# Gated attention stage: where the output projection is accumulated, and its place among the products

## The reference, cut to what matters

```python
def _L1_attn_ref(query, Wq, bq, Wk, bk, Wv, bv, Wu, bu, Wo, bo, ln_w, ln_b):
    q = jax.nn.relu(_heads(query @ Wq + bq))
    k = jax.nn.relu(_heads(query @ Wk + bk))
    v = _heads(query @ Wv + bv)
    u = query @ Wu + bu
    kv = jnp.einsum('bhnd,bhne->bhde', k, v)
    kv = _abs_clamp(kv)
    out = jnp.einsum('bhnd,bhde->bhne', q, kv)
    out = out.transpose(0, 2, 1, 3).reshape(query.shape)
    mu = jnp.mean(out, axis=-1, keepdims=True)
    var = jnp.var(out, axis=-1, keepdims=True)
    out = (out - mu) * jax.lax.rsqrt(var + EPS) * ln_w + ln_b
    out = u * out
    return out @ Wo + bo
...
x = x + _L1_attn_ref(_layernorm(x, axis=-1), ...)
```

## Time and profile before

| | us |
| --- | --- |
| median of 3 runs | 2989.97 (2986.45 to 2991.01) |
| the profiled execution | 2985.77 |
| its span in the trace | 2984.0 |
| PE busy in the span | 2905.4 (97%) |
| VectorE, ScalarE, GpSimd busy | 2340.0, 1729.2, 1743.0 |
| gated stage | about 2667 to 2867 in the trace |

### The profile page before, as it was taken

The page is one execution under the profiler, slowest core; times in us unless marked ns, Lnnn a source line. Parts: engine busy times, 40 slices in busy tenths (PEclk is TensorE's granted clock), DMA queues, the critical chain, the costliest instruction groups (busy, mean ns, idle before and its releaser), DMA issues.

```text
span 2984.0 us, 95481 instructions
## 1 busy us (share of the span) xinstructions
PE 2905.4 (97%) x34222; PEld 2534.5 (85%) x34222; DVE 2340.0 (78%) x6541; ACT 1729.2 (58%) x4568; POOL 1743.0 (58%) x1948
## 2 busy tenths in 40 slices
PE   6999999999999999999999999999999999999999
PEld 5888888878888888887888888878888888888888
DVE  6888887677778887888777787777777877887977
ACT  4777752267778324776777772247777622554355
POOL 7878740078888234334888861048888455627632
PEclk9999999999999999999999999999999999999999
DMA  4121121011211101000121112111211200000001
GB/s 143 45 75 42 47 82 37 27 33 41 71 40 43 49 21 44 11 12 23 36 71 40 41 47 72 35 29 40 69 42 43 65 22 14 29 0 1 1 15 43
DMA packets 178763, 122.65 MB, mean 41 GB/s; under 512 B 27532, under 2 KB 175336, under 8 KB 178024
## 3 DMA queue, kind: packets, MB, share of 16 engines
q1 hardware_dynamic: 177432, 117.77, 14.7%
q10 hardware_dynamic: 1104, 1.90, 0.2%
HBM read 48.29 MB, written 20.98 MB: 23 GB/s over the span
## 4 chain that ended last, share of the span: by engine, by line
PE 82%; DVE 6%; POOL 5%; issue 3%; SPq 1%; DMA 1%; ACT 1%; DVEq 0%; POOLq 0%; ACTq 0%
PE bank L406 7%; PE bank L408 7%; PE bank L407 7%; PE pair_bank L616 6%; PE scores L568 5%; PE scores L406 5%; PE scores L407 5%; PE scores L408 5%; PE bank L534 3%; PE pair_bank L406 2%; PE pair_bank L887 2%; PE pair_bank L886 2%; PE pair_bank L885 2%; PE scores L834 2%; PE scores L833 2%
## 5 line engine op out<-in xcount | busy, mean ns | idle before, releaser
L2956 POOL TENSOR_TENSOR prob<-prob,rsum 128x384 f32<-128x384 f32 x504 | 447.1, 914 | 226.6 <-DVE rsum L2114 226.6
L1395 ACT ACTIVATE prob<-prob,nmax 128x192 f32<-128x192 f32 x1024 | 451.9, 443 | 152.1 <-DVE nmax L2108 152.1
L1636 ACT ACTIVATE gate<-scores,bias 128x512 f32<-128x512 f32 x192 | 132.1, 688 | 499.3 <-PE scores L408 499.2
L2943 POOL TENSOR_TENSOR rn<-ss,mhalf 128x16 f32<-128x16 f32 x120 | 351.9, 2932 | 10.0
L406 PE MATMUL bank<-wqkv_hi,hT_hi 128*128 128x512 f32 x768 | 332.9, 434 | 7.3 <-DVE rot_t L2063 4.5
L2950 POOL TENSOR_TENSOR qk<-rot_t 128x512 f32<-128x512 f32 x256 | 322.5, 1280 | 12.2 <-DVE ss L2075 7.7
L2108 DVE CUSTOM_DVE_ANT_0 prob<-scores,masks,rn 128x192 f32<-128x192 f32 x768 | 267.4, 413 | 66.8 <-PE scores L568 65.3
L408 PE MATMUL bank<-wqkv_hi,hT_lo 128*128 128x512 f32 x768 | 304.2, 396 | 0.0
L407 PE MATMUL bank<-wqkv_lo,hT_hi 128*128 128x512 f32 x768 | 302.1, 393 | 0.0
L2924 POOL TENSOR_TENSOR rstd<-meanvar,eps 128x4 f32<-128x4 f32 x48 | 11.0, 229 | 486.3 <-DVE meanvar L2013 486.3
L406 PE MATMUL scores<-gT_hi,w_hi 128*128 128x512 f32 x576 | 227.6, 395 | 1.7 <-DVE gT_lo L2358 1.3
(11 more groups left out here) (415 smaller groups left out, 9562.9 us busy)
## 6 DMA issues: line engine op xcount, KB each, us to landing
Vlo<-V SPq DMA_DIRECT2D x256, 64.0 KB, 2.0
Vhi<-V SPq DMA_DIRECT2D x256, 64.0 KB, 2.0
H<-Y SPq DMA_DIRECT2D x128, 64.0 KB, 1.8
H<-ya SPq DMA_DIRECT2D x128, 64.0 KB, 1.9
yb<-Y SPq DMA_DIRECT2D x128, 64.0 KB, 1.6
HB<-Y SPq DMA_DIRECT2D x32, 256.0 KB, 2.8
HB<-yb SPq DMA_DIRECT2D x32, 256.0 KB, 3.0
raw<-in_L_ffn_wqkv SPq DMA_DIRECT2D x4, 1536.0 KB
```

The lines of the kernel that those rows point to most:

```text
L1395: e.activation(pb, pb, ACT.Exp, bias=nm[r][:, x:x + 1], scale=-1.0, accum_out=sums[r][:, x:x + 1]).then_inc(s_acEX[gi], 1)
L2943: e.tensor_tensor(rn[u][:, :], ss[u % 2][:, :], mhalf[:, :], ALU.pow).then_inc(s_plRN, 1)
L2956: e.tensor_tensor(pair, pair, rs[:, 2 * gi:2 * gi + 2].unsqueeze(2).to_broadcast([P, 2, KW]), ALU.mult).then_inc(s_plPN[gi], 1)
```

## The change

The projection of tiles 0 to 20 now goes into the right half (columns 256 to 511) of bank 6 or 7, the one that does not hold the product of its own parity, instead of bank 5. PE therefore waits ahead of it for `o_` of that bank's product instead of for `u_` and `X`; `u_` no longer waits for `X`; and `out_` of tiles 3 to 23 waits until VectorE has added the projection that lies in its bank. PE takes `kv` ahead of `out_`, and VectorE `kv` ahead of `stats2`. In turns after 33 PE takes `pr` ahead of `y_`'s transposes. VectorE keeps `pr` ahead of `stats2` up to turn 35 instead of 31.

```diff
         def last_product(T):
-            if T > FULL and T % 2:
+            if T <= FULL:
+                return bank[6 + (T + 1) % 2][:, D:2 * D]
+            if T % 2:
                 return bank[1 if T == FULL + 1 else 3][:, 0:D]
             return bank[5][:, 0:D]
...
                     if T == 0:
                         e.wait_ge(s_dvYB, U * GRP * (NRUN + 1) + OFF)
-                    e.wait_ge(z_dvX, NT + max(0, T - LAG1 - 2) + OFF)
                     of_tile(bank[5][:, 0:D], T, wug2).then_inc(g_peU, 1)
...
                     e.wait_ge(g_dvM, T - 1 + OFF)
+                    if 3 <= T <= FULL + 3:
+                        e.wait_ge(z_dvX, NT + T - 2 + OFF)
...
-                    e.wait_ge(z_dvX, NT + (T if T <= FULL else T - 1) + OFF)
+                    if T <= FULL:
+                        e.wait_ge(g_dvM, T + 2 + OFF)
                     if T == FULL + 1:
                         e.wait_ge(g_dvKV, NT + OFF)
+                    if T == FULL + 2:
+                        e.wait_ge(g_dvU, NT + OFF)
                     if T == FULL + 3:
                         e.wait_ge(g_dvC, NCL * B + OFF)
-                    e.wait_ge(g_dvU, min(NT, T + LAG1 + 3) + OFF)
+                    if T > FULL + 3:
+                        e.wait_ge(z_dvX, NT + T - 1 + OFF)
...
                     if is_tile(T + 1) and T:
                         tr(T + 1)
+                    if is_tile(T) and T:
+                        kv(T)
                     if is_tile(T - LAG1):
                         out_(T - LAG1)
-                    if is_tile(T) and T:
-                        kv(T)
+                    if is_tile(T - LAG1 - 2) and T > NT + 1:
+                        pr(T - LAG1 - 2)
                     if is_tile(T - LAG1 - 1):
                         y_(T - LAG1 - 1)
...
-                    if is_tile(T - LAG1 - 2):
+                    if is_tile(T - LAG1 - 2) and T <= NT + 1:
                         pr(T - LAG1 - 2)
...
-                    if is_tile(T - LAG1 - 3) and T < NT:
+                    if is_tile(T - LAG1 - 3) and T < NT + 4:
                         pr(T - LAG1 - 3)
+                    if is_tile(T):
+                        kv(T)
                     if is_tile(T - LAG1):
                         stats2(T - LAG1)
                         o_(T - LAG1)
-                    if is_tile(T - LAG1 - 3) and T >= NT:
+                    if is_tile(T - LAG1 - 3) and T >= NT + 4:
                         pr(T - LAG1 - 3)
-                    if is_tile(T):
-                        kv(T)
                     if is_tile(T):
                         u_(T)
```

## The result

The changed kernel took 2997.73 us, the median of 12 runs (2994.11 to 3001.79), against 2990.97 for the kernel before in the same sessions (12 runs, 2986.45 to 2993.53). The ratio is 1.0024, 95% interval 1.0016 to 1.0032: slower by 5 to 10 us, which is the side and the size that were predicted (+6.1 us, 2996.1; range 2989 to 3002). Its profiled run took 2999.9 us.

What follows compares the result with a forecast made beforehand. PE was taken to set the end, with VectorE seldom free. 2.7 us up to turn 30, 2.3 and 0.8 in the drain's first half and 0.3 in its second gave +6.1 us, 2996.1 us; range 2989 to 3002.

Steps and rivals of the forecast that it cites:

- turns without `q` (seven): Turns 13, 15, 19, 21, 23, 27, 29: projection stops waiting for `u_`, VectorE's chain then sets 4.40 us; -0.9 us.
- turn 11: Turn without a projection, now ending with the same VectorE chain as turns without `q`; +0.3 us.
- turns 16, 20, 24: Turns with `q` behind fresh statistics: `out_` waits for `X` of three tiles before, 6.87 instead of 6.00 us; +2.6 us.
- turns 14, 18, 22, 28: Turns that begin with transposes that waited, so `kv` starts 0.2 us late in each; +0.9 us.
- turn 17; turns 25 and 26: Turn 17: late `lo` hidden by `kv`, -0.5 us; 25 and 26: smaller clamp delay, two `Xn` delay `X`, +0.3 us.
- drain, first half: Turns 32 and 33: `out_` waits about 2.7 and 2.6 us for `X`, other stops go; +2.3 and +0.8 us.
- drain, second half: Projection ahead of `y_`'s transposes: stop of 0.3 us replaces one of 0.35; +0.3 us, bounds -2 and +2.
- The clock: Granted clock below 1.00 in the stage, named as something that would upset the sum; no size given.
- The waits simply go: Rival, PE's waits in the stage: `X` always in time, waits for `y` and `u` vanish; -6 to -9 us; chance 0.08.
- Half of it: Rival: new waits come, `y_` escapes GpSimd more often, drain's first `out_` waits 1.8 us; 0 to +6 us; chance 0.40.
- The new wait spreads: Rival: plain turns reach `X` 0.3 to 0.4 us late too, in some twelve turns; +9 to +12 us; chance 0.12.
- the rule on banks: PSUM: two engines must be kept apart by bank, so the wait on `X` stands; by columns the sum would be +0.4.

Runs made afterwards that it cites:

- e9: Changed kernel with nine matmuls, results unread, ahead of `out_` in turns 32 and 33 to fill PE's stops; ratio 1.0021.
- e7: Kernel before with `stats1` one turn earlier and nothing else; 2988.11 us, ratio 0.9995.
- e4: Kernel before with only the drain's part, the projection ahead of `y_`'s transposes in turns after 33; ratio 1.0001.
- e3: Changed kernel without the drain's part, the projection behind `y_`'s transposes there as before; ratio 1.0025.
- e11: Changed kernel with `stats1` one turn earlier, `X` ahead of `lo`, and the next layer's statistics and rows in even turns; 2991.34 us, ratio 1.0012.
- e1: Changed kernel with the old order, `out_` ahead of `kv` on PE and `kv` behind `stats2` and `o_` on VectorE; 3023.35 us, ratio 1.0111.
- e12: Kernel before with `stats1` one turn earlier, turn 34's stops filled with unread matmuls, next layer's first statistics in turns 20 and 21; 2985.75 us, ratio 0.9984.
- e2: Kernel before with the new order alone, `kv` ahead of `out_` and of `stats2`, projection still in bank 5; 2993.57 us, ratio 1.0011.

## Why the prediction was right, point by point

*Side and size.* +6.1 us predicted, +7.2 by the ratio (4.8 to 9.6). The trace's +9.1 splits like this (the drain's first half ends where `out_` of turn 35 starts, and 1.6 us of clock are taken out of it):

| term | predicted | measured |
| --- | --- | --- |
| turns without `q` (seven) | -0.9 | -0.75 (4.44 us, 4.40 predicted) |
| turn 11 | +0.3 | +0.3 |
| turns 16, 20, 24 | +2.6 | +3.15 (7.05 us, 6.87 predicted) |
| turns 14, 18, 22, 28 | +0.9 | +1.4 |
| turn 17; turns 25 and 26 | -0.5; +0.3 | -0.3; +0.6 |
| turn 12 | none | +0.25 |
| drain, first half | +3.1 | +2.6 |
| drain, second half | +0.3 | +0.3 |
| clock behind turn 33's stop | none | +1.6 |

The nearness of 6.1 to 7.2 is in part luck. Nearly all terms were set too low, as the table shows, and the clock was left out; against the trace the sum is 3 us short. With the clock held (e9) the trace's difference is +7.9. Why the ratio's 7.2 is less than either is open: the kernel before can lose its clock in the drain too, as e7 did with the same instructions there, and then less of it is left in the ratio.

*Turns 16, 20, 24.* The chain was right and two of its links short. I let `y_` take 0.60 us from start to start, since it would escape GpSimd; the rows above show 0.71, with GpSimd's product running from 2766.42 to 2767.16 and `y` until 2767.43. The step that failed in this term is that `y_` was taken to escape GpSimd. It never did: up to turn 32 it takes 0.77 to 0.90 us each time, and here it ends 0.27 us behind GpSimd's product. And `out_` behind its wait takes 0.52 to the next start, not 0.44. Together 0.19 a turn; the measured excess is 0.18.

*Turns 14, 18, 22, 28.* I gave all four the 0.2 of a late start. Turns 14 and 18 gained 0.23, but turns 22 and 28 grew by 0.48, because two `bn_stats` of the next layer stand ahead of `lo` there and `X` with it comes late too. PE's `out_` in turn 22:

```profile
2778.84 0.74 DVE L2015 BATCH_NORM_STATS2 stats<-X 128x6 f32<-128x256 f32 x2
...
2780.38 0.68 PE L1198 MATMUL pair_bank<-kvm,Y 128*128 128x128 f32 x4 [0.21 <-DVE X L2749]
```

Up to turn 30 the prediction had counted such instructions of the next layer only in turns 25 and 26.

*Drain.* `out_` of turn 32 stopped for 2.56 us (2.7 predicted) and that of turn 33 for 2.54 (2.6). The projection's wait of 0.6 for `y_low` didn't come, and that is most of the gap between 2.6 and 3.1. The lower clock hid it: in e9, with the clock held, PE does stop 0.23 us for `y_low` in turn 34, and `out_` of turn 35 starts 3.1 us later, counted from turn 30, than in the kernel before, which is the predicted 3.1. Counted so, the clock adds 1.1 and not 1.6. Of the second half the size was right in the split, but not the sign of the order in it: by itself it gains 0.15 (e4) to 0.3 us (e3 beside e9).

*The clock* was named as something that would upset the sum, without a price. The price was 1.6 us of PE's time and 1.1 at the end, and a long stop that the change itself makes stands right ahead of it. That the stop brings the fall is not shown: the clock also held behind such a stop, in e11.

*The rivals.* "The waits simply go" needed `X` in time; 12.3 us of waiting say it wasn't. "Half of it" had 0.40, and the lower end of the interval still reaches it (4.8 us), but the trace doesn't: its two conditions, an escaping `y_` and a first stop of 1.8 us, both failed. "The new wait spreads" failed as well: turns without `q` last 4.44, not 4.7, although `y_` was held in every one of them (0.78 us where it had been 0.85). Of the rule on banks no run here says more than the rows did: no kernel let two engines into one bank, so whether a half could be written earlier wasn't tried.

## What to carry over

Moving a result into another buffer does not remove a dependence, it chooses who waits for it: look up what stands ahead of the releaser in its own queue at the worst turn, not at the usual one. e1 shows the cost of asking only "which buffer is free". The same look at VectorE's queue, used to move the instructions that are in the way, gives 2.3 us in the trace of e7 and, with the next layer's statistics moved and the stops filled, a kernel that the runs can tell from before (e12, 0.9984). Test each half of a combined change alone, as one half can be there to pay for the other, and the half that pays can be better without it (e2).

## What the runs showed that was not expected

- The time at which the stage begins, in a program that is the same up to there, lay between 2670.6 us (e11) and 2677.5 us (e9) in the traces. That is a spread of 7 us, as large as the whole effect. It goes with the clock earlier in the program: the mean granted clock of the whole execution is 0.998 in e11 and 0.995 in e9, and over the first 100 us it is 0.97 and 0.93 (1.00 in the profile of before). The runs' times go with it too: 98 runs of the kernel before average 2986.8 us where that mean is 0.998 (15 runs), 2989.0 at 0.997 (45), 2991.6 at 0.996 (23) and 2993.5 at 0.995 (15). Comparing spans of two profiles would have said +14; counting from the stage's own start is what made terms of 0.3 us readable.
- With stops of 0.94 or 0.95 and 1.40 us within turn 34 the granted clock stayed at 1.00 in the kernel before and fell to 0.83 over 10 us in e7, with the same instructions around them; in e11 stops of 1.01 and 2.54 us left it at 1.00, in the changed kernel it fell behind stops of 2.56 and 2.54. The length of a stop alone does not tell. What else decides is open.
